# Two graph attention layers on one Trainium2 core: VectorE makes the low parts of the second layer's node rows one tile later in its order

## What is computed

```python
h = jnp.maximum(_layernorm(x, axis=-1), 0.0)
x = x + _L0_gnn_ref(h, adj, ...)
h = jnp.maximum(_layernorm(x, axis=-1), 0.0)
x = x + _L1_gnn_ref(h, adj, ...)
# each layer: Wh = h @ W + b;  e[i, j] = leaky_relu(Wh[i] @ a1 + Wh[j] @ a2, 0.2)
#             attention = softmax(where(adj > 0, e, -9e15), axis=1);  return attention @ Wh
```

## Time and profile before

| what | value |
|---|---|
| median of three runs | 2162.88 us |
| the profiled execution: its own time | 2164.1 us |
| its span, first to last instruction | 2162.2 us |
| mean granted TensorE clock | 0.990 |
| TensorE matmul busy | 1978.1 us (91%) |
| VectorE busy | 1774.1 us (82%) |
| ScalarE busy | 1133.4 us (52%) |
| GpSimd busy | 788.3 us (36%) |
| HBM, mean over the span | 165 GB/s |

### The profile page before, as it was taken

One profiled execution on the slowest core, in us unless ns is written; L12 is line 12 of the kernel. 1 busy time (PEld: TensorE's weight loads), 2 busy tenths in 40 slices (PEclk: granted clock), 3 DMA queues, 4 the chain that ended last, 5 costly groups with the idle time before them and its releaser, 6 DMA issues.

```text
span 2162.2 us, 46499 instructions
## 1 busy us (share of the span) xinstructions
PE 1978.1 (91%) x16866; PEld 1678.5 (78%) x16866; DVE 1774.1 (82%) x2733; ACT 1133.4 (52%) x1097; POOL 788.3 (36%) x819
## 2 busy tenths in 40 slices
PE   4557999999989999999999699999999999999998
PEld 2336778778777778878778588888888888888887
DVE  4668888888878888888889688888888888888885
ACT  3458778777767777778776332233223332333221
POOL 5654677666667667676765100000000000000000
PEclk9998999999999999999999899999999999999999
DMA  5549778778778778778775900000000000000000
GB/s 190 134 127 336 288 285 312 287 277 308 280 270 312 292 274 301 295 295 312 281 285 211 212 29 30 28 28 29 29 27 12 26 29 29 29 27 29 29 29 9
DMA packets 104788, 357.40 MB, mean 165 GB/s; under 512 B 12336, under 2 KB 61744, under 8 KB 67888
## 3 DMA queue, kind: packets, MB, share of 16 engines
q0 software_dynamic: 36864, 268.45, 32.6%
q1 hardware_dynamic: 65584, 71.73, 11.8%
q10 hardware_dynamic: 2304, 16.78, 2.4%
HBM read 314.84 MB, written 42.07 MB: 165 GB/s over the span
## 4 chain that ended last, share of the span: by engine, by line
PE 46%; issue 21%; DVE 11%; DMA 9%; POOL 5%; ACT 4%; DVEq 1%; POOLq 1%; SPq 0%; ACTq 0%
PE acc L583 45%; DMA adj_sb<-in_adj_dram,adj_index 6%; DVE masks L906 5%; POOL adj_sb L422 3%; ACT sign_a L645 2%; DMA node_rows<-row_parts 2%; ACT sign_z L658 1%; DVE ext L834 1%; DVE part_ac L933 1%; DMA mask_bytes<-pair_a 1%; POOL row_parts L469 1%; DMA masks<-in_x_dram 1%; DVE sign_z L853 1%; DVE centred L767 1%; DVE numer L952 1%
## 5 line engine op out<-in xcount | busy, mean ns | idle before, releaser
L583 PE MATMUL acc<-node_rows,masks 128*128 128x258 f16 x16384 | 1867.1, 274 | 50.4 <-DVE masks L913 21.4
L583 PEld LDWEIGHTS acc<-node_rows,masks 128*128 128x128 fp8e4 x16384 | 1601.9, 98 | 297.0 <-issue 52.3
L658 ACT ACTIVATE sign_z<-t_row,neg_s 128x2048 int8<-128x2048 f32 x256 | 503.0, 1991 | 2.0 <-DVE masks L906 1.9
L645 ACT ACTIVATE sign_a<-adj_sb 128x2048 int8<-128x2048 int32 x256 | 486.3, 1901 | 11.8 <-DMA adj_sb<-in_adj_dram,adj_index 11.6
L422 POOL DMA_INDIRECT adj_sb<-in_adj_dram,adj_index x256 | 443.1, 1731 | 81.1 <-issue 54.4
L664 ACT ACTIVATE part_a<-acc,coef_a 128x258 f32<-128x258 f32 x128 | 60.7, 474 | 685.0 <-PE acc L583 684.9
L853 DVE TENSOR_SCALAR sign_z<-t_row,neg_s 128x2048 int8<-128x2048 f32 x256 | 329.7, 1289 | 2.8 <-issue 2.2
L913 DVE TENSOR_SCALAR masks<-masks 128x2048 uint32<-128x2048 uint32 x256 | 311.8, 1218 | 0.3
L906 DVE STREAM_TRANSPOSE masks<-sign_z 128x2048 uint32<-128x2048 uint32 x128 | 295.0, 2305 | 0.1
L458 POOL TENSOR_TENSOR h_sum<-h_sum,ext 128x128 f32<-128x128 f32 x126 | 112.5, 893 | 315.8 <-DVE ext L834 312.0
L841 DVE SCALAR_TENSOR_TENSOR row_parts<-ext,b_and_d,row_parts 128x129 f16<-128x129 f32 x256 | 91.1, 357 | 149.2 <-POOL row_parts L469 121.1
(11 more groups left out here) (87 smaller groups left out, 691.0 us busy)
## 6 DMA issues: line engine op xcount, KB each, us to landing
node_rows<-row_parts SPq DMA_DIRECT2D x128, 129.0 KB, 7.2
node_rows<-node_rows SPq DMA_DIRECT2D x32, 516.0 KB, 11.8
mask_bytes<-pair_a ACTq DMA_DIRECT2D x16, 1024.0 KB, 5.0
pair_a<-mask_bytes SPq DMA_DIRECT2D x16, 1024.0 KB, 4.8
adj_sb<-in_adj_dram,adj_index POOLq DMA_INDIRECT x256, 8.7
x_old<-in_x_dram SPq DMA_DIRECT2D x64, 64.0 KB, 1.8
x_after_layer<-x_new SPq DMA_DIRECT2D x64, 64.0 KB, 1.5
x_old<-x_after_layer SPq DMA_DIRECT2D x64, 64.0 KB, 1.8
```

The lines of the kernel that those rows point to most:

```text
L583: mm = pe.matmul(acc[T.p][s][:, 0:ROW], stationary[s][:, c // BYTES, c % BYTES, :], node_rows[:, c, ROW * s:ROW * (s + 1)], start=(c == 0) ...
L645: nc.scalar.activation(sign_a[:, T.p, SPAN * r:SPAN * (r + 1)], adj_sb[:, r, :], ACT.Sign, scale=-1.0) \
L658: nc.scalar.activation(sign_z[:, T.p, SPAN * r:SPAN * (r + 1)], t_row[:], ACT.Sign, scale=-1.0, bias=neg_s[:, ds(RGROUPS * T.t + r, 1)]).t ...
```

## The change

In VectorE's iteration T of layer 0 both halves of `node_low` are called for tile T-3 and no longer for tile T-2. Their places among VectorE's other instructions stay the same. The sweep over layer 0 gets one more trailing iteration, since the last tile's low parts are now made in iteration 66; layer 1's trail stays 1. Nothing is changed on the other engines: their code, their waits and the counts are as before.

```diff
-                    ahead, done, before = T.plus(1), T.plus(-1), T.plus(-2)
-                    done_nodes, before_nodes = l == 0 and done.exists, l == 0 and before.exists
+                    ahead, done, before, earlier = T.plus(1), T.plus(-1), T.plus(-2), T.plus(-3)
+                    done_nodes, before_nodes, earlier_nodes = (l == 0 and of.exists for of in (done, before, earlier))
...
                     if done_nodes:
                         node_stats(1, done)
-                    if before_nodes:
-                        node_low(1, before, 0)
+                    if earlier_nodes:
+                        node_low(1, earlier, 0)
                     if done_nodes:
                         node_mean(1, done)
-                    if before_nodes:
-                        node_low(1, before, 1)
+                    if earlier_nodes:
+                        node_low(1, earlier, 1)
                     if done_nodes:
                         node_centre(1, done)
...
-                sweep(dve, tile, trail=2 - l, step=PACK)
+                sweep(dve, tile, trail=[3, 1][l], step=PACK)
```

## The result

The changed kernel takes **2139.55 us** (median of four runs, 2135.89 to 2143.12), against 2162.97 us of the kernel before in the same comparison. The ratio is 0.9888, with a 95% interval of 0.9868 to 0.9908: 1.1% faster. The prediction was 2098 us with a range of 2086 to 2125. The direction was right, the gain of 23 us is a third of the 65 us that were forecast, and the time lies outside the range.

The account below looks back on a forecast made before the run. VectorE was taken to bound layer 0, with TensorE next at 15.0 us a tile: 2164.1 - 68 for the sweep + 3 for the transition = 2099, and 1.2 lower for the median, 2098 us; range 2086 to 2125.

Parts of the forecast that it names:

- what bounded layer 0: Layer 0: VectorE is the bound at 16.13 us a tile; TensorE idles 1.15 us a tile behind it.
- the stall goes: VectorE's wait for GpSimd's high part, 2.05 us once a tile, falls to zero, leaving VectorE 14.01 us of work a tile.
- TensorE as the next bound: Layer 0: TensorE cannot follow VectorE's saving and sets the pace at 14.9 us a tile, between 14.84 and 14.98.
- The store of packed edges: Before `pack` in layer 0: landing in 4.2 to 10.7 us, median 5.0; cost kept at 6.6 us, 0.1 a tile.
- the transition: From layer 0 to layer 1: TensorE waits about 3 us (0 to 6) for the late reload.
- GpSimd: Layer 0: slower loads and high part make GpSimd the bound, 2123 to 2155 us; 0.04 in full, milder within a shared 0.24.
- the adjacency rows and the DMA engines: Layer 0: DMA rises to 315 GB/s; as rival, late rows give 15.3 to 15.6 us a tile, within a shared 0.24.
- the end of layer 0: SyncE's reload of groups 1 to 3 is issued from about 1209.5, not 1200.30; TensorE stands about 3 us.
- rival 3: Layer 0's stall only changes its name, to `part_a` or `ext`, and the late reload costs 6 to 10 us: 2172 us; 0.03.
- rival 4: The change does nothing: the wait moves to another semaphore and the reload is covered, 2164 us; chance 0.03.

Follow-up runs that it names:

- the late `pack`: Changed kernel with `pack` moved from VectorE's fourth place to the end of its iteration, after `node_centre`: 2082.75 us.
- the early store: Changed kernel with ScalarE issuing the store of packed edges one iteration earlier, after its second cast: 2083.27 us.
- the kernel in which `pack` fills the stall: Kernel before, with `pack` put just ahead of the second `node_low`, where VectorE stood still: 2125.8 us.
- the low parts put back: Changed kernel with low parts caught up in iterations 62 and 63: 2131.88 us; with `pack` also at the iteration's end: 2077.18 us.
- the kernel with the later store: Kernel before, with ScalarE issuing the store of packed edges after the copy of the transposed tile (line 620): 2257.76 us.

## Why the prediction was right or wrong

**Right: what bounded layer 0, and that the stall goes.** VectorE's 2.05 us a tile are gone, line 841 waits for nothing in the sweep, and TensorE no longer waits for `centred` there. Two of the signs did not come: TensorE was busy for 95% between 230 and 1100 us (829.6 of 870), not for over 98%, and VectorE waited for `part_a` only 12 times.

**Right, and too careful: TensorE as the next bound.** The forecast took 14.9 us for its tile, from 14.84 and 14.98. In the kernels without a stall it is 14.62. The 14.84 ran from TensorE's first matmul to ScalarE's answer, 0.2 us more than the tile. The 14.98 came from the busy time of tiles that all had a stop in them, 114.5 ns a matmul (873.10 us, 7622 of them), where the late `pack` without a stop has 111.8 (876.00 us, 7833). The timeline of before had the right value, from the same place of tile 62 to that of tile 63:

```profile
1178.16 3.74 PE L583 MATMUL acc<-node_rows,masks 128*128 128x258 f16 x32
...
1192.81 3.74 PE L583 MATMUL acc<-node_rows,masks 128*128 128x258 f16 x32
```

These are 14.65 us. The forecast gave TensorE's tile 0.28 us too much, which are 17 us over 60 tiles.

**Wrong: "The store of packed edges".** This is the step that failed. It took the store's landing times as a distribution, median 5.0 and sometimes more, that would stay the same when the schedule around it moved: "only the two or three stores above 6.5 us reach TensorE", 6.6 us in all. They are no distribution. Of the 15 stores before, 13 landed in 5.0 to 5.6 us and two in 9.7 and 10.7, and both late landings are of stores issued behind load r=1: the one issued at 612.21 us 0.98 us after the end of that load's issue (609.43 + 1.80), the one at 223.06 us 0.44 us after it. Each of the 13 is issued ahead of that end (871.47 against 872.12). After the change all 15 land as those two did. The rest of the step's working nearly holds: VectorE asks for the end some 5 us after the issue (4 were reckoned), waits 5.1 us, has 2.4 us in hand, and TensorE feels 2.9 us of it, 15 times. In the place of 6.6 us stands (15.52 - 14.62) x 60 = 54 us; the run with the late `pack` gave 57 us back. So the sum of the sweep was 1.13 us a tile where 0.61 was measured, and without this term it would have been 1.5.

Set against each other: 54 - 7 = 47 us too little for the store, 17 us too much for TensorE's tile, 2 us too little for the transition. That leaves 32 of the 37 us between 2099 and the 2135.9 us of the profiled execution; 1.3 us are lost before 211 us, 2.1 us in layer 1 beside the wait for the reload (934.5 us from TensorE's first matmul there to the end of the span, 928.9 before, less 3.5), and 1.5 us stay open.

**Right: GpSimd.** Its high part grew from 0.39 to 1.37 us in the median and its load r=2 from 0.94 to 1.88 us in the place shown; its wait for `ext` fell to 166.1 / 62 = 2.7 us, inside the 1 to 3 us named. It stayed covered: with the early store the high part took 1.47 us in the median, and TensorE was busy for 870.00 of 870 us beside it (230 to 1100 us). So as a rival for the time it fell here, though it did hold the kernel in which `pack` fills the stall. The rule of the Trainium skill (SBUF — State Buffer, on its two separate sides) that the prediction names agrees with these durations.

**Right: the adjacency rows and the DMA engines.** 315 GB/s were forecast for a pace that this kernel did not reach (303 GB/s). With the late `pack` 321 were reached, and ScalarE waited for adjacency rows for 2.0 us in all.

**Nearly right: the end of layer 0.** The reload was issued where it was forecast, 10 us after the first four, and TensorE's wait was 3.48 us, where "about 3 us" was said. What was missed is 1.6 us: the opening of layer 1 now takes 1199.62 - 1170.78 = 28.8 us from the last `finish_weigh`, and 1233.30 - 1206.05 = 27.2 us before. ScalarE's `node_high` of tile 63 waits for the store of tile 61's rows, and with the low parts put back that wait is gone and the opening is 27.5 us (1119.23 to 1146.70 in the run with the late `pack`). The wait was looked at in the sweep, where it is covered, but not at the end.

**The rivals.** Neither rival 3 nor rival 4, with no gain or a loss, came. What came is a wait that takes the place of the one removed. Rival 3 looked for it at `part_a` or at `ext`; it stands at the store, and it eats 0.90 of the 1.51 us a tile that the sweep could gain and not all of them.

## What to carry to other kernels

When an engine is sped up, list each DMA that another engine issues near it and ask which of them goes out first now and which would after; a landing time from the trace holds only for that order. A few landings that are twice as long as the rest are worth a look at what was issued just ahead of them: here the two late landings in the trace before showed what all 15 would become. Where one wait has two ends, the issue and the question, either can be moved: here each gave the same 57 us, without making anything faster. A wait for another engine that is filled with work may shrink by less than the work put in, when the other engine's instructions take longer beside that work: here 2.3 us of `pack` took 0.75 us off.

## What was not expected of the hardware

**A DMA's landing time jumps with the order of issue.** The 1 MB store takes 5.0 us when it is issued 0.65 us before the end of the issue of a 1 MB load on GpSimd's queue, and 9.9 us when it is issued 0.58 us after. With the early store, 1.6 us after the issue of load r=3 has ended, it is 5.8 us: of that load 0.83 MB still move in the first 2.00 us, none of the store beside them, and in the 3.10 us behind them the store moves 1.05 MB with 80% of the engines. The Trainium skill (DMA: Bandwidth & Descriptors, Queues, rings and completion order) says that each DMA engine goes round-robin between the queues that have work for it, and that it drains a whole packet from one before it switches, typically of 9 to 17 descriptors. An estimate from these figures: the store's data are 128 records of 8 KB over 16 engines, 8 for each, which could be one such packet. The trace agrees in this, that for some 4 us only one of the two transfers moves; no run shows where the packets end.

**A stall of TensorE can cost more than itself.** Of the 15 stalls of some 3 us in the changed kernel, 12 left the granted clock at 1.00 and three did not. The two others, of 3.37 and 4.38 us, were each followed by 18 matmuls in 4.03 us at a granted clock near 0.5. In this one TensorE stood for 3.65 us, and the next 18 matmuls took 3.47 us, not 2.17:

```profile
740.97 3.47 PE L583 MATMUL acc<-node_rows,masks 128*128 128x258 f16 x18 [3.65 <-ACT part_a L664]
```

The window around it (columns as above; the clock is 0.66 of full speed, so TensorE was at 1.2 GHz for part of it and at 2.4 GHz for the rest):

```profile
740.00:745.00 5.00, 4.03 (x22) 3.08 (x23) 4.82 (x12) 1.05 (x4) 4.48 (x4) 0.66 0.55 154
```

The same is seen after the wait for the last reload (28 matmuls in the first 4.7 us, clock 0.64), where part of layer 1's 2.1 us lies. It fits that the changed kernel's runs scatter by up to 11 us while those of the kernels without stalls scatter by 1 to 5. But the kernel with the later store has the longest stalls, and its four runs lie within 2.1 us, so what makes the scatter stays open.

**Empty instructions on ScalarE's queue delayed nothing.** 24 of them ahead of a DMA issue left it where it was, to 0.01 us, and the profile has a record of none.
